# Causal attention in half-blocks of 64 tokens in a fused two-layer kernel

## The reference

```python
h = rmsnorm(hidden, attn_norm_w)
q = (h @ q_w.T).reshape(B, S, 16, 128)      # 16 query heads
k = (h @ k_w.T).reshape(B, S, 4, 128)       # 4 key heads, each serves 4 query heads
v = (h @ v_w.T).reshape(B, S, 4, 128)
q, k = rope(rmsnorm(q, q_norm_w)), rope(rmsnorm(k, k_norm_w))
scores = einsum("bhqd,bhkd->bhqk", q, k) / sqrt(128)
scores = where(tril(ones(S, S)), scores, -inf)          # causal: S = 128
attn = einsum("bhqk,bhkd->bhqd", softmax(scores), v)
hidden = hidden + attn.reshape(B, S, 2048) @ o_w.T
```

## Time and profile before

| what | value |
|---|---|
| median of 3 runs | 1172.72 us (1172.37 to 1172.80) |
| the profiled execution's own time | 1174.76 us |
| its span | 1172.9 us |
| mean granted TensorE clock | 0.992 of full |
| busy: PE, weight loads, DVE, ACT, POOL | 97%, 87%, 62%, 55%, 43% |
| the second attention in the span | about 623 to 1060 us |

### The profile page before, as it was taken

The page is one execution under the profiler, slowest core; times in us unless marked ns, Lnnn a source line. Parts: engine busy times, 40 slices in busy tenths (PEclk is TensorE's granted clock), DMA queues, the critical chain, the costliest instruction groups (busy, mean ns, idle before and its releaser), DMA issues.

```text
span 1172.9 us, 22331 instructions
## 1 busy us (share of the span) xinstructions
PE 1141.4 (97%) x7602; PEld 1018.7 (87%) x7637; DVE 725.7 (62%) x1587; ACT 645.5 (55%) x1840; POOL 506.7 (43%) x566
## 2 busy tenths in 40 slices
PE   8999999999999999999999999999999999998995
PEld 7989999999999999998997788888888888877994
DVE  3666554334543454347777877777777787766556
ACT  4545543444444443455565766766766666674552
POOL 4111131113111311311336775675677588674573
PEclk9999999999999999999999999999999999999998
DMA  9200000000000002014002008930000100023747
GB/s 345 77 1 1 19 2 18 1 1 1 1 19 1 1 1 91 1 46 171 19 18 73 1 1 227 293 93 1 10 20 10 48 18 19 20 69 91 205 111 244
DMA packets 47265, 70.07 MB, mean 60 GB/s; under 512 B 4279, under 2 KB 39355, under 8 KB 46171
## 3 DMA queue, kind: packets, MB, share of 16 engines
q1 hardware_dynamic: 43475, 59.69, 16.8%
q0 software_dynamic: 3408, 8.43, 2.0%
q10 hardware_dynamic: 272, 0.52, 0.1%
HBM read 40.24 MB, written 29.30 MB: 59 GB/s over the span
## 4 chain that ended last, share of the span: by engine, by line
PE 89%; DVE 4%; issue 2%; ACT 2%; POOL 2%; DMA 1%; SPq 0%; POOLq 0%; DVEq 0%; ACTq 0%
PE bank L1878 15%; PE bank L1915 11%; PE bank L2068 10%; PE bank L1946 8%; PE bank L2122 7%; PE bank L1888 5%; PE bank L2213 5%; PE bank L1906 5%; PE bank L2148 4%; PE bank L2008 3%; PE bank L2256 3%; PE bank L2283 3%; PE bank L1896 2%; PE bank L2188 2%; PE bank L2178 2%
## 5 line engine op out<-in xcount | busy, mean ns | idle before, releaser
L592 POOL TENSOR_TENSOR p<-p,rinv 128x512 f32<-128x512 f32 x64 | 66.6, 1040 | 403.5 <-DVE rinv L1424 403.5
L946 ACT ACTIVATE p<-bank,nb,rq 128x128 f32<-128x128 f32 x256 | 113.8, 454 | 89.2 <-DVE nb L1647 89.2
L813 ACT ACTIVATE p<-bank,nmax 128x128 f32<-128x128 f32 x256 | 90.5, 366 | 115.6 <-DVE nmax L1412 115.4
L667 POOL TENSOR_TENSOR qr<-qr,rb 128x512 f32<-128x512 f32 x64 | 82.5, 1289 | 72.1 <-DVE rb L1601 70.6
L1420 DVE COPY pt<-bank 128x512 f32<-128x512 f32 x64 | 44.2, 691 | 106.0 <-PE bank L1896 105.4
L1878 PE MATMUL bank<-cur_hi,wqk_hi 128*128 128x512 f32 x256 | 107.8, 421 | 0.6 <-DVE cur_lo L1361 0.6
L1878 PE MATMUL bank<-cur_lo,wqk_hi 128*128 128x512 f32 x256 | 101.1, 395 | 0.0
L1878 PE MATMUL bank<-cur_hi,wqk_lo 128*128 128x512 f32 x256 | 100.9, 394 | 0.0
L822 ACT ACTIVATE o_hi<-bank,bqkv 128x512 fp32r<-128x512 f32 x64 | 44.2, 690 | 95.9 <-PE bank L1906 95.5
L1428 DVE SCALAR_TENSOR_TENSOR o_lo<-bank,bqkv,o_hi 128x512 fp32r<-128x512 f32 x64 | 48.0, 750 | 49.6 <-ACT o_hi L822 49.6
L1915 PE MATMUL bank<-wo_hi,o_hi 128*128 128x256 f32 x256 | 77.7, 303 | 0.3 <-DVE o_lo L1428 0.2
(11 more groups left out here) (274 smaller groups left out, 3652.4 us busy)
## 6 DMA issues: line engine op xcount, KB each, us to landing
token_scratch<-empty SPq DMA_DIRECT2D x1, 17415.0 KB, 64.8
xs<-token_scratch SPq DMA_DIRECT2D x39, 129.0 KB
wqk_raw<-in_wqk SPq DMA_DIRECT2D x8, 512.0 KB, 9.8
gate<-gates_scratch SPq DMA_DIRECT2D x8, 512.0 KB, 3.8
got_t<-expert_scratch SPq DMA_DIRECT2D x16, 256.0 KB, 4.8
w_raw<-in_w SPq DMA_DIRECT2D x2, 1408.0 KB, 6.0
xres<-in_x SPq DMA_DIRECT2D x4, 512.0 KB, 8.9
wv_raw<-in_wv SPq DMA_DIRECT2D x8, 256.0 KB, 10.0
```

The source lines that it names most:

```text
L592: nc.gpsimd.tensor_tensor(p1[:, h % 2], p1[:, h % 2], rinv[:, h % 2].unsqueeze(2).broadcast_to([P, GB, T]), ALU.mult).then_inc(a_pn, 1)
L667: nc.gpsimd.tensor_tensor(qr[:, s.u % 2], qr[:, s.u % 2], rb[:], ALU.add).then_inc(g_qr, 1)
L813: last = nc.scalar.activation(p1[:, h % 2, b], bank[3][:, b * T:(b + 1) * T], ACT.Exp, bias=nmax[:, h % 2, b:b + 1], accum_out=rsum[:, h % ...
L946: last = nc.scalar.activation(p2[:, (s.u - 3) % 2, j], bank[3][:, j * T:(j + 1) * T], ACT.Exp, scale=rq[:, (s.u - 3) % 4, j:j + 1], bias=n ...
```

## The change

The 128 queries of a head are cut into two halves of 64. `q_t` is reordered so that a block of 128 columns holds the same half of two heads: blocks 0 and 1 the first halves (heads 0 and 1, heads 2 and 3), blocks 2 and 3 the second halves. A first half needs only keys 0 to 63, so the products of blocks 0 and 1 have 64 moving columns in place of 128. The mask shrinks to the two triangles: two products of 128 columns in place of one of 512. Keys 64 to 127 of blocks 0 and 1 are filled once with -1e30 by a DVE `memset` (semaphore `g_pad`). The reordering is done in two ACT copies (L967, L972) and in DVE's L1692, by access patterns. As a partition now belongs to different tokens and heads, epsilon is added by four DVE instructions that also move the sums of squares between the halves of the partitions; they stand behind `o_lo` in DVE's order. POOL's instruction L690 and its two waits go; POOL's L694 waits for the last of the four.

```diff
-        mask = sb("mask", [P, REP * T], BF16, at=W2 + 45 * KB)
+        mask = sb("mask", [P, 2, HALF], BF16, at=W2 + 45 * KB)
+        def by_head(t):
+            return t[:].rearrange("p (h j t) -> p j h t", h=2, j=REP)
+        def in_order(t):
+            return t.rearrange("p (j h t) -> p j h t", h=2, j=REP)
+        def blocks(t):
+            return t[:].rearrange("p (c s) -> p c s", s=T)
...
 # POOL, step
-                    pool.wait_ge(g_ss, n + 1)
-                    if s.had(2):
-                        pool.wait_ge(g_rq, n - 1)
-                    nc.gpsimd.tensor_tensor(q_ve[:, s.u % 2], q_ms[:, s.u % 2], eps[:, 0:REP], ALU.add).then_inc(g_qv, 1)
                     pool.wait_ge(g_qv, n + 1)
...
 # ACT, step
-                    nc.scalar.activation(o2_hi[:], bank[6][:], ACT.Copy).then_inc(g_oh, 1)
+                    nc.scalar.activation(in_order(o2_hi[:]), by_head(bank[6]), ACT.Copy).then_inc(g_oh, 1)
...
-                    nc.scalar.activation(q_t[:, (s.u - 1) % 2], bank[4][:], ACT.Copy).then_inc(g_qt, 1)
+                    nc.scalar.activation(by_head(q_t[:, (s.u - 1) % 2]), in_order(bank[4][:]), ACT.Copy).then_inc(g_qt, 1)
...
 # DVE, once
-                            nc.vector.tensor_copy(mask[:].rearrange("p (j s) -> p j s", j=REP),
-                                                  mask_f[:].unsqueeze(1).broadcast_to([P, REP, T])).then_inc(g_tab, 1)
+                            for i in range(2):
+                                ps = slice(i * HALF, (i + 1) * HALF)
+                                last = nc.vector.tensor_copy(mask[ps], mask_f[ps, i].unsqueeze(1).broadcast_to([HALF, 2, HALF]))
+                            last.then_inc(g_tab, 1)
...
+                    nc.vector.memset(blocks(bank[3])[:, 0:2, HALF:T], -1e30).then_inc(g_pad, 1)
...
 # DVE, step
-                    nc.vector.tensor_tensor(o2_lo[:], bank[6][:], o2_hi[:].bitcast(F32), ALU.subtract).then_inc(g_ol, 1)
+                    nc.vector.tensor_tensor(in_order(o2_lo[:]), by_head(bank[6]), in_order(o2_hi[:].bitcast(F32)),
+                                            ALU.subtract).then_inc(g_ol, 1)
+                if s.new():
+                    dve.wait_ge(g_ss, n + 1)
+                    for a, b in ((0, 0), (0, 1), (1, 1), (1, 0)):
+                        last = nc.vector.tensor_scalar(q_ve[b * HALF:(b + 1) * HALF, s.u % 2, 2 * a:2 * a + 2],
+                                                       q_ms[a * HALF:(a + 1) * HALF, s.u % 2, b::2], EPS, None, ALU.add)
+                    last.then_inc(g_qv, 1)
...
 # PE, step
-                    pe.matmul(bank[3][:], ident_b[:], mask[:], start=True, stop=False, skip_group_check=True)
+                    if s.first and s.u == 2:
+                        pe.wait_ge(g_pad, 1)
+                    for i in range(2):
+                        pe.matmul(blocks(bank[3])[:, 2 * i:2 * i + 2, i * HALF:(i + 1) * HALF], ident_b[:], mask[:],
+                                  start=(i == 0), stop=False, skip_group_check=True)
                     for j in range(REP):
-                        js = slice(j * T, (j + 1) * T)
-                        last = pe.matmul(bank[3][:, js], q_t[:, s.u % 2, js], k_t[:, slot, kv * T:(kv + 1) * T],
+                        keys = (1 + j // 2) * HALF
+                        last = pe.matmul(bank[3][:, j * T:j * T + keys], q_t[:, s.u % 2, j * T:(j + 1) * T],
+                                         k_t[:, slot, kv * T:kv * T + keys],
                                          start=False, stop=(j == REP - 1), skip_group_check=True)
```

More of the change, by code:

```diff
@@ L49 @@
 CAP = B * T
+HALF = T // 2
 ROWS = E * CAP + (E - 1) * P
@@ L168, in program @@
         cos_sin = sb("cos_sin", [P, 2, DH], at=W2 + 44 * KB)
-        mask = sb("mask", [P, REP * T], BF16, at=W2 + 45 * KB)
+        mask = sb("mask", [P, 2, HALF], BF16, at=W2 + 45 * KB)
         ident_b = sb("ident_b", [P, P], BF16, at=W2 + 46 * KB)
-        mask_f = sb("mask_f", [P, T], at=W2 + 46 * KB + 256)
+        mask_f = sb("mask_f", [P, 2, HALF], at=W2 + 46 * KB + 256)
         small = W2 + 46 * KB + 768
@@ L310, in program @@
             sem(f"g_{x}") for x in ("ka", "rk", "kv", "qr", "rq", "qv", "pn"))
+        g_pad = sem("g_pad")
         w_hi4, w_lo4 = sem("w_hi4"), sem("w_lo4")
@@ L624, in _ @@
             nc.gpsimd.affine_select(out=mask_f[:], in_=mask_f[:], compare_op=ALU.is_ge, fill=-1e30, base=0,
-                                    pattern=[[-1, T]], channel_multiplier=1).then_inc(consts, 1)
+                                    pattern=[[-HALF, 2], [-1, HALF]], channel_multiplier=1).then_inc(consts, 1)
             for g in range(NG - 1):
@@ L1621, in step @@
                     h_rest(NG * NF - 1, NF - 1, False)
+                    dve.wait_ge(n_ev, 2 * (3 * NG - 1))
+                    nc.vector.memset(blocks(bank[3])[:, 0:2, HALF:T], -1e30).then_inc(g_pad, 1)
                 if s.first and s.u == 14:
```

## The result

The changed kernel takes 1197.51 us, median of 4 runs (1195.66 to 1199.03); the kernel before took 1172.76 beside it (1172.37 to 1174.03). The ratio is 1.0205, 95% interval 1.0193 to 1.0218: some 24 us slower, and far outside the predicted range. Each such difference is known to 1.1 to 3.2 us, by the 95% interval beside it.

A forecast was written before the change was run, and what follows sets the result against it. PE was taken to bound the second attention. PE's -3.6 us, stalls +3.55 and POOL -0.5 gave about -0.6 us against 1172.72, so 1172.1 us; range 1167.8 to 1175.3 us.

The forecast's parts named there:

- PE's part: Mask and scores on PE: split mask saves 0.06 us, half-size scores 0.015, together 0.07 a step; 52 steps give -3.6 us.
- The rival by columns: PE's score records: time follows columns alone, 0.33 us a step saved, 20 us, 1153 us after some stalls; chance 0.04.
- The four by themselves: DVE's four new instructions behind `o_lo`, ahead of the next `nmax`: 0.15 us each, 0.6 us a step.
- the rule on held instructions: On DVE, an instruction starting in another quadrant than the one before waits for all earlier ones; three of four held.
- So four cost between 0.32 and 0.84 us.: DVE's four a step, bounded by start spacings of small instructions: 0.08 us with nothing between, 0.21 with a wait.
- The slower rival: DVE takes over the pace, `nmax` behind the four: +1.6 us at 0.84, about +4 (1176.7) if waiting for POOL's `p`; chance 0.21.
- For keys L675 comes later too ... and the key transposes have about 1.9 us there: nothing.: POOL's L675 for the keys: at worst 1.1 us later, about 1.9 us of room at the key transposes, so no cost.
- stalls: DVE's 0.6 us unhidden: group 0 2.0 us, group 3 steps 1 and 2 1.1, before the drain 0.45; sum 3.55 us.
- POOL's -0.5 us in the ramp-up: POOL loses 64 instructions of 0.2 us, counting only in two ramp-up steps where the chain runs through POOL: -0.5 us.
- what would show it right: Signs: score records 0.11 us apart, mask to scores 0.16, step 5.59, the four 0.6, PE's `p` waits about 8 us.

The follow-up runs named there:

- PE's part alone: Changed kernel with POOL adding the queries' epsilon in one instruction as before, in place of DVE's four (half the rows wrongly scaled): ratio 0.9981, -2.2 us.
- 0.6 us of DVE alone (before, four reduces): Kernel before, with four `tensor_reduce` of 64x2 added on DVE behind `o_lo`, writing to a place nobody reads: ratio 1.0063, +7.4 us.
- both of these, `rk` first: Changed kernel with DVE's four as `tensor_reduce` (epsilon left out) and POOL's keys' `rk` computed ahead of the queries' `rq`: ratio 1.0044, +5.2 us.
- with the lock, `rk` first: Changed kernel, DVE's four still `tensor_scalar`, with POOL computing the keys' `k_ve` and `rk` ahead of its wait for `q_ve`: ratio 1.0123, +14.4 us.
- with the late `rk`, no lock: Changed kernel with DVE's four as `tensor_reduce` in place of `tensor_scalar`, same place, epsilon left out, `rk` still behind `rq`: ratio 1.0099, +11.6 us.

## Why the prediction was wrong

| kernel | us against before |
|---|---|
| PE's part alone | -2.2 |
| 0.6 us of DVE alone (before, four reduces) | +7.4 |
| both of these, `rk` first | +5.2 |
| with the lock, `rk` first | +14.4 |
| with the late `rk`, no lock | +11.6 |
| with both: the changed kernel | +24.0 |

Taken alone the lock is worth 14.4 - 5.2 = 9.2 us and the order 11.6 - 5.2 = 6.4; together they make 24.0 - 5.2 = 18.8. The 3 us above their sum may come from their meeting, a delayed `rk` behind delayed four, but four measured times stand behind this figure, each known to 1.5 to 3 us, so it isn't shown. Even with both taken away the change costs 5.2 us, 1178 us, and that is outside the predicted range too.

**PE's part: right, a little large.** Predicted 0.07 us a step (mask 0.06, scores 0.015); measured 0.05, none of it by fewer columns of scores, -2.2 us in place of -3.6. That a float32 record is not shorter than its load held: eight records of either size start 0.11 us apart. The rival by columns is out. How the 0.05 comes about was not foreseen: the first scores start 0.11 us behind the mask, not 0.16, and the eight records then last 0.87 us to the projection where they had lasted 0.81. The prediction had read 0.89 for them before, from the chain, which counts another stretch.

**The four by themselves: right.** Predicted 0.6 us from the first to what follows; where POOL is idle they take 0.68, and `nmax` starts 0.08 before their end. Their spacing is (0.63 - 0.15)/3 = 0.16 us for the reduces, against the 0.08 of unheld ones. So the rule on held instructions, which the prediction cited from the Trainium skill ("VectorE: DVE Perf Modes", Two Vector instructions with no wait between them), agrees with this trace.

**The failing step, first: "So four cost between 0.32 and 0.84 us."** The upper bound was for instructions that meet nobody. Beside POOL's elementwise instructions they waited till those were over, up to 2.49 us. The slower rival had this ("if they must also wait for POOL's running `p`"), with 0.4 us and about +4 us in all. Of the changed kernel's 64 groups 27 lasted over 0.9 us, and the lock alone is worth 9.2 us. The Trainium skill ("SBUF — State Buffer", section "SBUF: two separate sides") gives the rule: a DVE instruction in a 2-port mode, or one with two SBUF inputs against a GpSimd one that reads SBUF, and the GpSimd instruction exclude each other for the whole instruction. The traces agree, with `nb` at 2.33 us beside POOL's add of 2.33, and reduces that never waited. And the trace of the kernel before showed it; I had read means. Its DVE and POOL:

```profile
1044.38 0.65 DVE L1647 TENSOR_TENSOR nb<-nmax,rq 128x4 f32<-128x4 f32 x1
1049.17 0.16 DVE L1647 TENSOR_TENSOR nb<-nmax,rq 128x4 f32<-128x4 f32 x1
1044.05 1.83 POOL L709 TENSOR_TENSOR w_lo<-w_raw,w_hi 128x352 fp32r<-128x352 f32 x2 [0.59 <-ACT w_hi L1000]
```

The same instruction takes 0.16 us or 0.65, and the slow one overlaps POOL.

**The failing step, second: "For keys L675 comes later too ... and the key transposes have about 1.9 us there: nothing."** The late `rk` was seen and its size was about right. The follower was the wrong one. Ahead of the transposes it is DVE itself that waits for `rk`, in order, with both rotations, `q_ms`, `o_lo`, the four and `xres` queued behind. DVE's wait for `rk` went from 3.6 to 11.9 us, and PE's for `xres` to 9.8. Putting `rk` first gave 9.6 us back.

**A term mis-sized: stalls.** Predicted 3.55 us for 0.6 us a step; four reduces in the kernel before cost 7.4 (4.6 to 10.2). The places were largely right. By the start of the scores that run loses 2.7 us in group 0 (predicted 2.0) and 1.5 in the first steps of group 3 (predicted 1.1). Some 0.5 us are lost at the start of group 1 and again of group 2, where I had counted nothing, and 1.8 us in the first drain step, where PE waits 1.64 us for `p` in place of 0.32; I had given it 0.45. The last scores start at 1054.81 us in place of 1047.28, so by then the 7.4 us are complete.

**POOL's -0.5 us in the ramp-up** was not seen. The scores of step 4 start 0.27 us earlier than before in the run with PE's part alone, with POOL's instruction still there; with reduces on DVE, none on POOL and `rk` first they start 0.01 us later.

**The clock** was no step of the prediction. It adds to the loss in the profiled execution of the changed kernel, by the estimated 2 and 1.7 us above. From 645 to 650 us it is 0.52 to 0.91 in all five runs with `tensor_scalar` on DVE, and 1.00 in the five with reduces (in the kernel before with four reduces PE had waited 1.68 us); so a part of what is called the lock's share is the clock's. It is not the loss itself: of the four executions two had a mean granted clock of 0.994 and 0.993, no lower than the 0.992 of the kernel before's profiled execution, and still took 1195.66 and 1196.08 us. The two with 0.989 took some 3 us more.

Of what would show it right, half came true: score records 0.11 us apart, and PE's wait for `p`, 8.6 us with the plain four reduces for the 8 foreseen. The changed kernel's own 9.7 us is near too, but by luck: four that stand still and a late `rk` were not in that figure. The first scores came 0.11 us behind the mask in place of 0.16, and the four took about 0.6 us only where POOL was idle. The list had no sign for a wait on `xres`.

## What to carry to other kernels

When DVE gets a small instruction in fp32 from SBUF to SBUF, or with two SBUF inputs, look at what POOL runs at that moment, and compare the longest of such instructions in the trace with the mean; the `tensor_reduce` of this case, with one input, didn't wait. When a helper engine is made to wait for another one, go through its queue behind the wait, and for each entry ask which engine stops first for it, not who uses the data last; if a result is needed only steps later, make it a step late, at the place where the engine stands idle anyway. All three together (the reduce, `rk` first, a step late) turned +24 us into -2.8.

## What the runs showed of the hardware

- Small DVE instructions of two forms stood still while POOL ran. A `tensor_scalar` of 128x4, f32 in SBUF, took 0.16 us alone, 0.47 on average beside POOL and 1.95 at most; four of 64x2 took 0.68, 1.11 and 2.49. A `tensor_tensor` of 128x4 with two SBUF inputs took 0.16 alone and up to 2.33. Four `tensor_reduce` of 64x2 took 0.63 either way.
- Float32 products with 64 moving columns in four of eight records took the same time as with 128 in all, 0.98 us for mask and records either way.
- Small instructions that write to the other half of the partitions start 0.16 us apart on DVE; on ACT four take 0.84 us.
- The same change came to +24.0, +44.3 or, as reduces a step later with `rk` first, -2.8 us, by the place and form of four small instructions and by POOL's order.
